# A windowed-attention and spectral-filter kernel: the forward transform's even frequencies from sums and differences of two quarters of the rows

## The reference, cut to what matters

```
def _stu_conv(phi, u, n):                      # n = 8192, u: (b, sl, d)
    Vf = jnp.fft.rfft(phi, n=n, axis=0)
    Uf_p = jnp.fft.rfft(u, n=n, axis=1)
    Uf_m = jnp.fft.rfft(u * sgn3, n=n, axis=1)
    U_plus = jnp.fft.irfft(Vf[None, :, :, None] * Uf_p[:, :, None, :], n=n, axis=1)[:, :sl]
    U_minus = jnp.fft.irfft(Vf[None, :, :, None] * Uf_m[:, :, None, :], n=n, axis=1)[:, :sl]
    ...
out = jnp.einsum('btkd,k,kde->bte', U_plus, s, Mpp)
out = out + jnp.einsum('btkd,k,kde->bte', U_minus, s, Mpm)
...
for i, frac in enumerate((1, 2, 4, 8)):
    xi = x[:, :T // frac]
    si = _stu(xi, sigma, phi, M_u[i], M_phi_plus[i], M_phi_minus[i])
```

## Time and profile before

| | |
|---|---|
| three executions | 2104.64, 2109.42, 2111.65 us (median 2109.42) |
| the profiled execution | 2103.28 us, of which the span of instructions is 2102.0 us |
| TensorE, share of the span | 93% |
| VectorE, ScalarE, GpSimd | 55%, 52%, 29% |
| mean granted clock of TensorE | 0.972 |
| the forward transform's matmuls | 512 records of L1120, 64 of L1109 |
| the stretch | about 828 to 1040 us |

### The profile page before, as it was taken

The page is one execution under the profiler, slowest core; times in us unless marked ns, Lnnn a source line. Parts: engine busy times, 40 slices in busy tenths (PEclk is TensorE's granted clock), DMA queues, the critical chain, the costliest instruction groups (busy, mean ns, idle before and its releaser), DMA issues.

```text
span 2102.0 us, 64958 instructions
## 1 busy us (share of the span) xinstructions
PE 1948.0 (93%) x27483; PEld 1407.5 (67%) x27483; DVE 1162.9 (55%) x3209; ACT 1095.6 (52%) x2122; POOL 610.5 (29%) x780
## 2 busy tenths in 40 slices
PE   4898898888899877999999999999999999999998
PEld 2566666565666655665577777777777777767776
DVE  2566667777766664142256666666665656544332
ACT  4678777667776553322455555555555555510000
POOL 5344445445544432020132222222222122100000
PEclk8899999999999997999999999999999999999999
DMA  4332323323232224348612221222212222386551
GB/s 97 90 85 66 95 69 82 93 70 87 66 96 79 77 57 117 73 132 178 198 41 59 59 59 43 55 59 53 55 37 52 59 59 58 81 222 178 158 155 47
DMA packets 281600, 183.63 MB, mean 87 GB/s; under 512 B 55416, under 2 KB 279360, under 8 KB 279520
## 3 DMA queue, kind: packets, MB, share of 16 engines
q1 hardware_dynamic: 278942, 178.99, 32.6%
q10 hardware_dynamic: 2304, 0.40, 0.2%
q0 software_dynamic: 64, 0.08, 0.0%
HBM read 108.87 MB, written 70.63 MB: 85 GB/s over the span
## 4 chain that ended last, share of the span: by engine, by line
PE 69%; DVE 10%; ACT 6%; issue 6%; POOL 4%; DMA 3%; SPq 2%; DVEq 0%; ACTq 0%; POOLq 0%
PE banks L1278 19%; PE banks L1261 19%; PE banks L1443 9%; PE banks L1120 7%; PE banks L383 4%; DVE zone L582 3%; ACT zone L526 2%; DVE st L569 2%; PE banks L342 2%; PE banks L377 1%; DVE W L622 1%; ACT L526 1%; DMA Ud<-kP 1%; POOL zone L802 1%; PE banks L332 1%
## 5 line engine op out<-in xcount | busy, mean ns | idle before, releaser
L1311 DVE COPY Gm<-banks 128x896 f32<-128x896 f32 x448 | 488.3, 1091 | 348.0 <-PE banks L1261 348.0
L1297 ACT ACTIVATE Gm<-banks 128x896 f32<-128x896 f32 x448 | 412.1, 920 | 318.0 <-PE banks L1261 313.3
L1261 PE MATMUL banks<-V,zone 118*128 118x224 bf16 x3584 | 438.1, 261 | 1.9 <-ACT qT L1132 0.6
L1278 PE MATMUL banks<-Gm,U 128*32 128x128 f32 x12544 | 434.9, 276 | 3.9 <-issue 2.6
L1261 PEld LDWEIGHTS banks<-V,zone 118*128 118x128 bf16 x3584 | 291.9, 98 | 125.1 <-issue 44.8
L1278 PEld LDWEIGHTS banks<-Gm,U 128*32 128x32 f32 x12544 | 316.3, 110 | 85.4 <-issue 84.1
L1326 POOL COPY U<-UL 128x896 f32<-128x896 f32 x28 | 50.4, 1800 | 637.2 <-PE banks L1278 495.2
L1443 PE MATMUL banks<-YC,zone 98*98 98x256 f32 x1024 | 226.5, 379 | 0.7 <-DVE YC L1500 0.7
L1443 PEld LDWEIGHTS banks<-YC,zone 98*98 98x98 f32 x1024 | 168.7, 165 | 53.5 <-DVE YC L1500 1.6
L839 POOL TENSOR_TENSOR W<-W,mx 128x280 f32<-128x280 f32 x196 | 128.8, 657 | 244.9 <-DVE mx L629 244.4
L1120 PE MATMUL banks<-XR,W 98*128 98x392 f32 x512 | 175.7, 501 | 6.3 <-DVE W L1145 4.2
(11 more groups left out here) (142 smaller groups left out, 2285.5 us busy)
## 6 DMA issues: line engine op xcount, KB each, us to landing
Yd<-YS SPq DMA_DIRECT2D x112, 224.0 KB, 4.3
W<-Vd SPq DMA_DIRECT2D x392, 49.0 KB
UL<-Ud SPq DMA_DIRECT2D x28, 448.0 KB, 4.4
zone<-Yd SPq DMA_DIRECT2D x32, 392.0 KB
YL<-Yd SPq DMA_DIRECT2D x32, 392.0 KB
zone<-Mbf SPq DMA_DIRECT2D x28, 256.0 KB
Vd<-W SPq DMA_DIRECT2D x112, 56.0 KB
T<-XR SPq DMA_DIRECT2D x28, 224.0 KB, 3.5
```

The lines of the kernel that those rows point to most:

```text
L1261: ins = e.matmul(pt[:, q, :], self.M[:, par, 64 * half + 4 * i + q, :], self.V[P % 2][:, par, :], start=True, stop=True)
L1278: ins = e.matmul(p[32 * x:32 * x + 32, :], self.U7[(2 * P + ch) % 3][:, sl, 8 * (3 - q):8 * (3 - q) + 32], self.Gm[:, par, r:r + 2, :], st ...
L1297: e.activation(dst, src, ACT.Copy).then_inc(S["gm_act"], 1)
L1311: v.tensor_copy(dst, src).then_inc(S["gm_dve"], 1)
```

## The change

The even frequencies are ordered by their remainder of four: first 0, 4, 8, ..., then 2, 6, 10, .... For these, row j and row 391-j of `EV` (and of `OD`) have table values equal up to sign, so the sum runs over two blocks of 98 rows in place of four, after a fold. The second half of `EV` and `OD` is now built in reversed row order (from `UR` and the reversed `UA`), so that the fold pairs blocks that lie at the same partitions. VectorE makes four more tiles `fold[c, h]` for each window, of 98x512: sum and difference of the halves of `EV` and of `OD`. A piece of `blk` 0 then consists of two groups (h) of two accumulating matmuls of 196 frequencies each, in the two halves of the bank's 392 columns. `blk` 1 keeps four matmuls of 392. `fold` is a single buffer: before it is written, VectorE waits for j3 of the window before. j0 waits for `folded` instead of `evod`. The table `F` has 4704 columns instead of 6272, and all tables by frequency follow the new order.

```
@@ Spectrum.__init__
-        self.F = XR[0:G, 7:21, :].rearrange("p a b -> p (a b)")[:, 0:6272].rearrange("p (c a x) -> p c a x", c=2, a=4)
+        x = XR[0:G, 7:21, :].rearrange("p a b -> p (a b)")
+        self.F = x[:, 0:4704]
+        self.Fodd = self.F[:, 0:3136].rearrange("p (c a x) -> p c a x", c=2, a=4)
+        self.Fev = self.F[:, 3136:4704].rearrange("p (c h a x) -> p c h a x", c=2, h=2, a=2)
+        self.fold = x[:, 4704:6752].rearrange("p (c h a x) -> p c h a x", c=2, h=2, a=2)
@@ Spectrum.tensor
+            src = (self.UR, self.UA)[a][w % 2]
             for x in range(2):
-                ins = e.matmul(p[0:G, 256 * x:256 * x + 256], self.rev[:, :], self.UR[w % 2][:, 3 - 2 * a - x, :], start=True, stop=True)
+                ins = e.matmul(p[0:G, 256 * x:256 * x + 256], self.rev[:, :], src[:, 3 - x, :], start=True, stop=True)
...
-                e.wait_ge(S["evod"], 2 * w + 2)
+                e.wait_ge(S["folded"], w + 1)
...
-            for a in range(4):
-                ins = e.matmul(p[:, 0:392], src[:, a, 128 * m:128 * m + 128], self.F[:, c, a, 392 * half:392 * half + 392],
-                               start=a == 0, stop=a == 3)
+            ms = slice(128 * m, 128 * m + 128)
+            if blk == 0:
+                for h in range(2):
+                    for a in range(2):
+                        ins = e.matmul(p[:, 196 * h:196 * h + 196], self.fold[:, c, h, a, ms], self.Fev[:, c, h, a, :],
+                                       start=a == 0, stop=a == 1)
+            else:
+                src = (self.EV, self.OD)[c][w % 2]
+                for a in range(4):
+                    ins = e.matmul(p[:, 0:392], src[:, a, ms], self.Fodd[:, c, a, :], start=a == 0, stop=a == 3)
@@ Spectrum.vector
-            v.tensor_tensor(self.EV[w % 2][:, 2 * a:2 * a + 2, :], self.UA[w % 2][:, 2 * a:2 * a + 2, :], pv, ALU.add)
-            v.tensor_tensor(self.OD[w % 2][:, 2 * a:2 * a + 2, :], self.UA[w % 2][:, 2 * a:2 * a + 2, :], pv, ALU.subtract
-                            ).then_inc(S["evod"], 1)
+            if a == 0:
+                v.tensor_tensor(ev[:, 0:2, :], ua[:, 0:2, :], pv, ALU.add)
+                v.tensor_tensor(od[:, 0:2, :], ua[:, 0:2, :], pv, ALU.subtract).then_inc(S["evod"], 1)
+                return
+            v.tensor_tensor(ev[:, 2:4, :], ur[:, 0:2, :], pv, ALU.add)
+            v.tensor_tensor(od[:, 2:4, :], pv, ur[:, 0:2, :], ALU.subtract).then_inc(S["evod"], 1)
+            v.wait_ge(S["evod"], 2 * w + 2)
+            if w:
+                v.wait_ge(S["dft"], 8 * w - 4)
+            v.tensor_tensor(self.fold[:, 0, 0], ev[:, 0:2, :], ev[:, 2:4, :], ALU.add)
+            v.tensor_tensor(self.fold[:, 0, 1], ev[:, 0:2, :], ev[:, 2:4, :], ALU.subtract)
+            v.tensor_tensor(self.fold[:, 1, 0], od[:, 0:2, :], od[:, 2:4, :], ALU.subtract)
+            v.tensor_tensor(self.fold[:, 1, 1], od[:, 0:2, :], od[:, 2:4, :], ALU.add).then_inc(S["folded"], 1)
@@ tables
-    even = np.arange(0, 784, 2)
+    even = np.concatenate([np.arange(0, 784, 4), np.arange(2, 784, 4)])
```

More of the change, by code:

```diff
@@ L1113, in tensor @@
             blk, m, c = j // 4, j // 2 % 2, j % 2
-            half, src = c ^ blk, (self.EV, self.OD)[c][w % 2]
             if j == 0:
-                e.wait_ge(S["evod"], 2 * w + 2)
+                e.wait_ge(S["folded"], w + 1)
             self.wait_slot(e, SPECTRUM_USE[w, 2 + j])
             p = self.slot(SPECTRUM_USE[w, 2 + j])
-            for a in range(4):
-                ins = e.matmul(p[:, 0:392], src[:, a, 128 * m:128 * m + 128], self.F[:, c, a, 392 * half:392 * half + 392],
-                               start=a == 0, stop=a == 3)
+            ms = slice(128 * m, 128 * m + 128)
[8 more added lines that the diff above has]
+                    ins = e.matmul(p[:, 0:392], src[:, a, ms], self.Fodd[:, c, a, :], start=a == 0, stop=a == 3)
             ins.then_inc(S["dft"], 1)
@@ L1143, in vector @@
             pv = self.slot(SPECTRUM_USE[w, a])[0:G, :].rearrange("p (a x) -> p a x", a=2)
-            v.tensor_tensor(self.EV[w % 2][:, 2 * a:2 * a + 2, :], self.UA[w % 2][:, 2 * a:2 * a + 2, :], pv, ALU.add)
-            v.tensor_tensor(self.OD[w % 2][:, 2 * a:2 * a + 2, :], self.UA[w % 2][:, 2 * a:2 * a + 2, :], pv, ALU.subtract
-                            ).then_inc(S["evod"], 1)
+            ev, od, ua, ur = (x[w % 2] for x in (self.EV, self.OD, self.UA, self.UR))
+            if a == 0:
[11 more added lines that the diff above has]
+            v.tensor_tensor(self.fold[:, 1, 1], od[:, 0:2, :], od[:, 2:4, :], ALU.add).then_inc(S["folded"], 1)
     def sync(self, e, k, n):
@@ L1173, in sync @@
                         ).then_inc(S[f"d_ud{blk}"], 16)
-SPECTRUM_SIGNALS = "d_fwd d_u0 d_u1 d_ud0 d_ud1 revmm evod dft fu".split()
+SPECTRUM_SIGNALS = "d_fwd d_u0 d_u1 d_ud0 d_ud1 revmm evod folded dft fu".split()
 def load_spectra(e, D, S, c):
@@ L1615, in tables @@
     NP_, J = 1568, 784
-    even = np.arange(0, 784, 2)
+    even = np.concatenate([np.arange(0, 784, 4), np.arange(2, 784, 4)])
     odd = np.arange(1, 784, 2)
     slots = np.concatenate([even, odd])
-    j = np.arange(392)[:, None] + 0.5
+    near = np.arange(196)[:, None] + 0.5
+    rows = np.concatenate([near, 392 - near])
     th = lambda a, f: 2 * np.pi * a * f / NP_
[L1621 to L1627, removed]
+    fo = odd[None, :].astype(float)
+    fi = even[None, :].astype(float)
+    fodd = np.stack([-np.sin(th(rows, fo)), np.cos(th(rows, fo))]).reshape(2, 4, 98, 392).transpose(2, 0, 1, 3)
+    fev = np.empty((2, 2, 2, 98, 196))
+    for h in range(2):
+        f = fi[:, 196 * h:196 * h + 196]
+        top = f.copy()
+        if h == 0:
+            top[0, 0] = 784.0
+        fev[0, h] = np.cos(th(near, f)).reshape(2, 98, 196)
+        fev[1, h] = -np.sin(th(near, top)).reshape(2, 98, 196)
+    fwd = np.concatenate([fodd.reshape(98, 3136), fev.transpose(3, 0, 1, 2, 4).reshape(98, 1568)], 1)
     jj = np.arange(784)[:, None].astype(float)
```

## The result

The changed kernel takes 2098.27 us (median of 10 runs, 2091.21 to 2104.1), the kernel before 2110.53 beside it (10 runs, 2103.34 to 2119.11). The forecast was 22.6. The sign was right and the gain too large: from the 2109.42 on which the forecast was built, the ratio gives 2095.7 us, where 2086.8 was forecast and 2070 to 2098 was the range; the new median by itself lies 0.3 us above that range.

What follows compares the result with a forecast made beforehand. TensorE was taken to bound the kernel until window 3 ends, then a fixed DMA transfer list; 17.4 us (earlier weights) plus 5.2 (window 7) gave 22.6, so 2109.4 - 22.6 = 2086.8 us, range 2070 to 2098.

Steps and rivals of the forecast that it cites:

- The narrow record: Even-frequency matmuls: a 196-column record takes 166 ns instead of 329, saving 41.8 us of TensorE over 256 records.
- The fourth rival: Even matmuls: load and stream add up, 356 ns a record instead of 329, so the kernel gets slower, 2116.2 us; chance 0.05.
- The folds at w0: First window of the forward transform: VectorE's four extra sums lie wholly on the path and delay TensorE by 2.5 us.
- The standstill at w6: Window 6, first odd piece: TensorE stands still some 16 us (2.04 before), until batch 2's Ud<-kP store lands.
- the savings of w4 to w6: Windows 4, 5 and 6: their shorter matmuls (5.2 us a window) gain nothing, as TensorE waits for the unchanged DMA list.
- I let this cost 1 us: VectorE's work before the first weights: two more folds cost 1 us, so the weights start 17.4 us earlier, near 945.9.
- the second rival: Front's tail: waits on Un stores (9.9 us) are added again, weights only 7.5 us earlier, gain 12.7 us, 2096.7; chance 0.20.
- The 12.9 us in that paragraph: How much earlier VectorE begins its work of 908.3 to 959.4 us: 15.7 from windows 0 to 2, less 2.5, rounded.
- Behind that point nothing waits anew: After the standstill in window 6: the Ud<-qT store and window-7 load keep their distance to Ud<-kP, adding no wait.
- from there all is as before: From the last Ud<-kP store, issued at 1007.5 instead of 1030.12, the rest runs unchanged, keeping the whole 22.6 us.
- w7: Last window of the forward transform: its even part is the only other saving behind the standstill, 5.2 us.
- the first rival: TensorE stays the bound to the end, the kP store landing by 970 us; all savings count, 39.3 us, 2070; chance 0.12.

Runs made afterwards that it cites:

- e5: Changed kernel with the last batch's spectra in two idle front buffers, so window 6 waits for no batch-2 store: 2100.6 us, ratio 0.9937 to the kernel before.
- e4: Changed kernel without VectorE's four folds, even pieces reading EV and OD directly (even frequencies not the reference's): 2093.89 us, ratio 0.9907 to the kernel before.
- e1: Changed kernel run again with no edit: 2099.51 us, ratio 0.9940 to the kernel before; its profiled run took 2112.64 us.
- e6: Changed kernel with the folds of windows 1 to 7 on GpSimd instead of VectorE: 2096.91 us, ratio 0.9911 to the kernel before.
- e3: Kernel before, with weight groups 1 and 2 behind batch 2's Ud<-qT store, group 3 behind the second row load: 2121.55 us, ratio 1.0035.
- e2: Changed kernel, weight groups 1 and 2 behind batch 2's Ud<-qT store, group 3 behind the second row load: 2091.44 us, ratio 0.9894 to the kernel before.
- e7: Changed kernel, weight group 1 behind batch 2's Ud<-qT, group 2 behind last Ud<-kP and first row load, group 3 behind second row load: 2091.49 us, 0.9882.
- e11: Kernel before, with weight group 1 behind batch 2's Ud<-qT store, groups 2 and 3 behind the second row load: 2121.01 us, ratio 1.0034.
- e9: Changed kernel, weight group 1 behind batch 2's Ud<-qT store, groups 2 and 3 behind the second row load: 2086.36 us, ratio 0.9870 to the kernel before.

## Why the prediction was right in sign and too large

Right, point by point:

- **The narrow record.** 166 ns forecast, 166 measured. The fourth rival (356 ns) is out, and with it, for this kernel, the rule of the Trainium skill (TensorE: Matmul & The Clock Gate, where it stands under The mechanism) that it followed: all loads fill the same rows, and they overlap. The group of loads that feeds L1129 (busy us, mean ns of one) shows 199 ns each under a pace of 166:

```profile
L1129 PEld LDWEIGHTS banks<-XR 98*128 98x128 f32 x256 | 44.8, 199 | 12.3 <-DVE XR L1170 11.5
```

- **The folds at w0.** 2.5 us forecast, 6.78 - 4.25 measured.
- **The standstill at w6.** About 16 us forecast, 14.27 measured; a ScalarE wait "from 10.7 to about 25 us", 17.74 measured: the wait began at 970.9, not near 961. From the start of the weights to the landing of Ud<-kP it took 38.0 us (988.6 - 950.66), forecast 39.8; the 1.9 us less than in the kernel before were not forecast, and are luck. That the savings of w4 to w6 are swallowed by the list of transfers holds, and e5 shows it: with the wait for that store gone TensorE stood just as long at the next load.

Too small by 2.9 us: **"I let this cost 1 us"**, VectorE between w2 and the batch's end. The weights came 14.5 us earlier, not 17.4. VectorE's timeline shows where: w4's four folds stand in its order before the sum that feeds the T and Un stores, and that sum starts as the last fold ends.

```profile
932.13 0.68 DVE L684 TENSOR_TENSOR XR<-XR,banks 112x512 f32<-112x512 f32 x1
...
946.04 1.11 DVE L582 TENSOR_SCALAR zone<-XR,zone 112x128 f32<-112x128 f32 x4 [6.83 <-DMA Un<-zone]
```

SP's T store follows at 932.84, and the twiddle loads, Un stores and weights keep their old distances behind it within 0.6 us. e4, without the folds, gives the price from the other side: 4.0 us behind w0, where 1 was allowed. The time is that of the second rival in small, its mechanism isn't: that rival wanted longer waits on Un stores, and these came to 8.4 us (0.38, 1.21 and 6.83) for 9.9 before. (The 12.9 us in that paragraph should be 13.2, 15.7 less 2.5; nothing further hangs on it.)

**The step that failed:** "Behind that point nothing waits anew", and with it "from there all is as before". The last Ud<-kP was issued 20.5 us earlier (22.6 forecast), which would have been nearly the whole forecast: 14.5 from the weights, 1.9 from the shorter list, 4.1 where 5.2 were forecast for w7, mostly since the restart is slower (5.59 us for 4.59). Two things took from it.

1. *The landing and the rows.* The store came 18.6 us earlier; SP was done with issuing the second pair of weight groups at 992.3, where it was 1006.8 in the kernel before, 14.5 us earlier. So the store follows the weights more closely, and how long the engines need for the weights differs from run to run. Five microseconds of the kernel before, a little ahead of its store's issue at 1030.12, then the same five microseconds in the changed kernel and in e1 (us, TensorE busy with records, granted clock, DMA share, GB/s):

```profile
1025.00:1030.00 5.00, 5.00 (x17) 1.00 0.14 46
```
```profile
1005.00:1010.00 5.00, 5.00 (x31) 1.00 0.45 105
```
```profile
1005.00:1010.00 5.00, 5.00 (x16) 1.00 1.03 161
```

In the kernel before the engines are nearly idle when the store comes. In the changed kernel they are only coming free, and in e1, where SP ended at 1000.5, they stay nearly full until 1025. The store landed 7.4 us after its issue in the low profile, 8.8 in e6, 11.7 in e4, 12.2 in e3, 12.5 in e5 (there from qT), 14.3 in e1 and 17.1 in e2, where 5.1 was assumed; in e7 to e11, where groups 2 and 3 come behind it, it is 5.1 to 5.2 again. Such a list was in the prediction, for the first two weight groups (39.8 us), and was missing for the second two. From their issue to the landing of the last Ud<-kP it took 42.5 us in the kernel before, 39.7 in the changed one, 42.8 in e4 and e6, 46.4 in e1. Worked out from the forecast's own times, as an estimate in hindsight: these groups issued at 945.9 + 29.5 = 975.4, and 39.8 us more give 1015.2, later than the 1012.6 at which the store was to land. Why the weights pass more slowly in one run than in another stays open.

Behind the landing there is a chain with a fixed length: first row load 3.9 us, GpSimd 7.7, second load, GpSimd again, 23.2 us from 1018.94 to the matmul at 1042.15. In the kernel before it was 23.1 us (from 1035.26), and TensorE waited 1.07 us for it. That one row, the second below, said that there was no reserve, and I had not looked at it. SP's queue and TensorE in the kernel before:

```profile
1035.26 0.61 SPq L1191 DMA_DIRECT2D UL<-Ud  x1
...
1058.37 0.86 PE L1278 MATMUL banks<-Gm,U 128*32 128x128 f32 x24 [1.07 <-POOL U L1338]
```

Any delay of the landing is then paid one for one: 3.42 us of waiting in the low profile, 9.5 in the high one. A table of TensorE in the 50 us behind the first filter matmul (start and end, us, busy with records, granted clock, DMA share, GB/s), of before, of the changed kernel, and of e1 (there 0.5 us later):

```profile
1039.50:1089.50 50.00, 47.04 (x841) 1.00 0.29 85
```
```profile
1021.00:1071.00 50.00, 44.72 (x793) 1.00 0.31 92
```
```profile
1028.70:1078.70 50.00, 38.62 (x585) 0.83 0.26 78
```

Of the same work, 48 records fewer are done in the one and 256 in the other. In e1 the clock is lower too: TensorE had stood before, and its matmuls at L1302 take 1.51 us for 24 records, not 0.86.

2. *The inverse.* 247.8 us from its first matmul to the end, 244.0 in the kernel before: 3.8 us, with the same work. Over all profiles it lies between 243.8 and 251.0 for the changed kernels and 244.0 and 248.4 for those of before, so I take it for spread between runs. Its cause stays open.

The sum closes: -18.5 for the first filter matmul (1021.00 for 1039.54), +2.6 for the filters (821.1 us for 818.5, the wait for rows in it), +3.8 for the inverse give -12.1, the difference of the spans; with the late start of 1.9 us taken off it is 14.0. So of the 8.6 us that this pair of profiles lacks to the forecast 22.6, 2.1 were lost ahead of the store's issue and 2.6 in the filters, the step that failed; the largest part, 3.8, is the unexplained inverse. The failed step weighs more in other runs: with the weights in their old place the filters take 822.4 us in e6, 825.2 in e4, 825.3 in e5 and 834.5 in e1. What it costs in the median was not measured by itself.

e2, e7 and e9 show the failed step from the other side. Each keeps the change and moves weights out of the way of what is waited for; each gains (0.9894, 0.9882, 0.9870 instead of 0.9935), and each time the longest new waits stand with what is still behind weights (in e9 that is argued, not shown). With the stores and the first rows ahead of groups 2 and 3 in both kernels the change is worth some 35 us, near the 39.3 of the first rival, which needed just this: that the stores don't lie behind the weights. The prediction gave it 0.12 and was right that the kernel as it stands does not meet it.

Not settled: what the folds cost in the whole time (e4's 5.6 us with overlapping intervals), what the rests in e9 are, whether GpSimd is the better place for the folds (e6), and the inverse's spread.

## What to carry to other kernels

When a faster engine makes an issue earlier, ask what is still in flight on the DMA engines at the new time: a store that landed in 5 us may land in 15 behind a bulk load that has not moved as far. Then follow the chain behind the landing to the first wait on the bounding engine, however short; a wait of 1 us there says that the chain has no reserve, and every delay is paid in full. And once a change has turned compute into waiting, try the order of the transfers again: the same order that loses 0.3% on the old kernel wins some 0.6% on the new one (0.9870 and 0.9935, each against the kernel before on its own chip).

## What was not expected of the hardware

- With the DMA share near 1 in both, the rate was 163 GB/s in the stretch in which the first weights pass, and 345 GB/s between 978 and 989.5 us of the changed kernel, up to the landing of Ud<-kP. The share tells that the engines are occupied, not what they move.
- After 14.27 us of rest TensorE began at a granted clock of 0.50: 5.59 us for what otherwise takes 2.63. A standstill costs its length and here some 3 us more.
- Runs of the changed kernel spread over 24 us (2088.46 to 2112.64), and the point where TensorE begins to wait for w0's sums lies between 831.6 and 841.5 us among all profiles, though no step ahead of it differs. Two single profiles are best laid over each other at such a mark before any times are subtracted.
